# Self-attention on one core: the order of ScalarE's last copies in a unit

## The reference, cut to what matters

```
q, k, v = xn @ Wq1, xn @ Wk1, xn @ Wv1      # 16 heads of 64
attn    = softmax(q k^T * 64**-0.5)         # 512 x 512 for each head
x       = concat_heads(attn @ v) @ Wo1 + bo1 + x
```

## Time and profile before

| | |
|---|---|
| time of 3 runs | 2262.8, 2264.51, 2266.3 us; median 2264.51 |
| profiled execution | 2263.67 us, of which its span (first to last instruction) is 2261.8 us |
| busy share of the span | PE 94%, DVE 71%, ACT 66%, POOL 47% |
| self-attention | about 543 to 1718 us of the span |

### The profile page before, as it was taken

One profiled execution on the slowest core, in us unless ns is written; L12 is line 12 of the kernel. 1 busy time (PEld: TensorE's weight loads), 2 busy tenths in 40 slices (PEclk: granted clock), 3 DMA queues, 4 the chain that ended last, 5 costly groups with the idle time before them and its releaser, 6 DMA issues. The chain is left out here.

```text
span 2261.8 us, 31322 instructions
## 1 busy us (share of the span) xinstructions
PE 2117.4 (94%) x11628; PEld 1768.1 (78%) x11628; DVE 1602.4 (71%) x2349; ACT 1487.3 (66%) x2157; POOL 1066.5 (47%) x830
## 2 busy tenths in 40 slices
PE   6868999998999999999999999999997799999998
PEld 4657888887777777777777777777776788998887
DVE  5576777755787777877877778777785866666553
ACT  5546888766777777777777777777774354555431
POOL 3155444431454454554544545445454666565432
PEclk9979999999999999999999999999999899999999
DMA  6810000021000100001000010010004411111000
GB/s 209 304 44 5 22 22 22 17 76 38 25 15 16 38 15 25 25 15 34 15 25 24 15 34 15 16 34 15 26 29 168 137 58 44 50 57 47 10 10 20
DMA packets 84280, 102.67 MB, mean 45 GB/s; under 512 B 29664, under 2 KB 61152, under 8 KB 83616
## 3 DMA queue, kind: packets, MB, share of 16 engines
q1 hardware_dynamic: 84128, 100.66, 13.5%
HBM read 65.50 MB, written 33.82 MB: 44 GB/s over the span
## 5 line engine op out<-in xcount | busy, mean ns | idle before, releaser
L146 PE MATMUL PS<-R 128*128 128x512 f32 (+1 forms) x2944 | 1021.6, 347 | 60.0 <-DVE R L162 25.1
L147 PE MATMUL PS<-R 128*128 128x512 f32 (+1 forms) x2944 | 994.1, 338 | 0.0
L148 PE MATMUL PS<-R 128*128 128x512 f32 (+1 forms) x2944 | 994.0, 338 | 0.0
L146 PEld LDWEIGHTS PS<-R 128*128 128x128 f32 x2944 | 561.7, 191 | 171.2 <-issue 37.4
L156 ACT ACTIVATE R<-PS 64x512 fp32r<-64x512 f32 (+4 forms) x860 | 460.4, 548 | 230.6 <-PE PS L1840 127.7
L148 PEld LDWEIGHTS PS<-R 128*128 128x128 f32 x2944 | 560.9, 191 | 60.6
L147 PEld LDWEIGHTS PS<-R 128*128 128x128 f32 x2944 | 562.0, 191 | 56.1
L162 DVE TENSOR_TENSOR R<-F,R 128x1024 fp32r<-128x1024 f32 (+2 forms) x418 | 462.9, 1112 | 38.0 <-POOL R L159 22.6
L159 POOL TENSOR_SCALAR R<-F 128x512 fp32r<-128x512 f32 (+1 forms) x293 | 264.0, 903 | 259.5 <-DVE F L1997 147.3
L1535 ACT ACTIVATE F<-PS 128x1024 f32<-128x1024 f32 x256 | 263.0, 1028 | 170.6 <-DVE R L162 112.3
L159 POOL TENSOR_SCALAR R<-R 64x512 fp32r<-64x512 f32 x128 | 142.6, 1129 | 391.3 <-ACT R L156 391.3
(11 more groups left out here) (92 smaller groups left out, 1992.4 us busy)
## 6 DMA issues: line engine op xcount, KB each, us to landing
F<-sd SPq DMA_DIRECT2D x128, 128.0 KB, 2.9
xs<-F SPq DMA_DIRECT2D x16, 512.0 KB, 2.6
F<-xs SPq DMA_DIRECT2D x16, 512.0 KB, 3.5
gd<-F SPq DMA_DIRECT2D x8, 768.0 KB, 3.9
vd<-F SPq DMA_DIRECT2D x8, 768.0 KB, 6.4
R<-gd SPq DMA_DIRECT2D x6, 1024.0 KB, 5.6
R<-vd SPq DMA_DIRECT2D x6, 1024.0 KB, 5.9
F<-in_x SPq DMA_DIRECT2D x8, 512.0 KB, 5.0
```

The lines of the kernel that those rows point to most:

```text
L146: nc.tensor.matmul(o, L[0], Rr[0], start=start, stop=False, skip_group_check=share)
L147: nc.tensor.matmul(o, L[0], Rr[1], start=False, stop=False, skip_group_check=share)
L148: return nc.tensor.matmul(o, L[1], Rr[0], start=False, stop=stop, skip_group_check=share)
```

## The change

ScalarE's two copies of the values' accumulators, with their wait for `o3_lo` of the unit before, move behind the two negating copies of the maxima with theirs. Nothing is added or removed, and no other engine's stream changes.

```diff
                         act_copy(OB[64:65, :], bank(4)[64:65, :])
                         act_copy(OB[0:1, :], bank(5)[0:1, :]).then_inc(d3_sum.sem, 1)
-                        act.wait_ge(o3_lo, d - 1)
-                        act_copy(OA[0:64, :], bank(4)[0:64, :])
-                        act_copy(OA[64:128, :], bank(5)[64:128, :]).then_inc(d3_out.sem, 1)
                     if ok(u, N3) and j == 3:
                         act.wait_ge(nm3_mm, u)
                         act.wait_ge(c3_mm, 4 * (u - 2) + 3)
                         act.wait_ge(k3_clear, u % 2)
                         for h in range(2):
                             m = act_copy(qb[u % 2][h][64:65, :], bank(odd_bank(u))[64 * h:64 * h + 1, :], scale=-1.0)
                         m.then_inc(nm3_neg.sem, 1)
+                    if ok(d, N3) and j == 3:
+                        act.wait_ge(o3_lo, d - 1)
+                        act_copy(OA[0:64, :], bank(4)[0:64, :])
+                        act_copy(OA[64:128, :], bank(5)[64:128, :]).then_inc(d3_out.sem, 1)
```

## The result

| | before | after |
|---|---|---|
| median of the runs | 2264.95 us (4 runs, 2262.8 to 2266.3) | 2291.88 us (4 runs, 2290.51 to 2294.24) |
| ratio | | 1.0115, 95% interval 1.0103 to 1.0127 |
| span of the profiled execution | 2261.8 us | 2288.8 us |

The change costs 27 us, 1.2%. Forecast were 20.5 us, 0.9%. All of it arises in the self-attention: from the second end of a step to the 62nd (60 steps) the timelines take 1108.3 us before and 1135.7 us after.

What follows compares the result with a forecast made beforehand. TensorE was taken to bound the self-attention, VectorE's chain behind E0 being a hidden second bound. Output ends 10.5, late plain ends 9.2 and the rest 0.75 made +20.5 us: 2284.8 us, forecast 2278 to 2292, 8-in-10 range 2268 to 2294.

Steps and rivals of the forecast that it cites:

- What bounds the kernel: Self-attention: TensorE is busy 1099 of 1140 us; VectorE, almost without a pause behind ScalarE's copies, is the hidden second bound.
- The gain at L1385: TensorE's weight load at plain ends waits for ScalarE's maxima; the change can win 0.35 us there.
- Plain ends with late transposes: 20 ends, transposes ending 1.57 to 1.84 us behind the row sums' start: E0 +0.50, TensorE +0.37; 0.46 us taken each.
- margin of L1419: Late plain ends: 0.1 to 0.3 us read between the rests of k and the TensorE matmul that needs them.
- Output ends: 30 ends: `values` +0.24 to +0.37 us on TensorE, E0 +0.36 meeting slack on VectorE's chain; 0.35 us taken each.
- Plain ends with early transposes: 10 ends where ScalarE never idles: TensorE wins 0.4 us and gives it back; 0 to +0.1, 0.05 us taken each.
- The sum: All ends of the self-attention together: 10.5 + 9.2 + 0.75 = 20.5 us slower.
- A: Faster: ScalarE's slack swallows E0's delay; plain ends win 0.35 us each, output ends lose nothing: -11 us, 2254; chance 0.06.
- B: Near nothing: only TensorE's direct wait counts, VectorE's delay of L1419 perhaps meeting a wider margin; +4.4 us, 2269; chance 0.17.
- high end of the sum: E0's shift counts in full at every end: 30 x 0.49 + 20 x 0.62 + 10 x 0.1 = 28.1 us.
- C: Lags add up: `values` and VectorE's chain both cost in each unit, or GpSimd's part moves; +28 to +34 us; chance 0.15.
- The price from the Trainium skill: ScalarE's copies priced by rule at 613 ns, step 520: the two pairs end 0.2 us sooner, estimate about +12 us.

Runs made afterwards that it cites:

- E0: Not a run: ScalarE's work that starts behind the q copies; at late plain ends 4.73 us after the row sums' copies start before, 5.37 in the changed kernel.
- e3_chain: Before, with one more 512-element ScalarE copy (0.6 us) ahead of the q copies behind 58 of the 62 ends; 2299.38 against 2264.39 us.
- e4_direct: Before, with the accumulators' semaphore d3_out raised by the next step's first q copy and no copy moved; 2272.13 against 2264.39 us.
- e5_dve: Before, with the accumulators copied by VectorE in its idle time instead of ScalarE, TensorE also waiting for d3_sum; 2266.99 against 2265.74 us.
- e1_plain: Before, with the change made at the 31 plain ends alone, output ends keeping ScalarE's old order; 2278.54 against 2264.39 us.

## Why the prediction was right, point by point

- **What bounds the kernel.** VectorE's run as the hidden second bound, fed by ScalarE's E0, is what the runs showed; it was underrated. It bounds the steps behind both kinds of ends. The run is not quite unbroken: VectorE waits 0.26 us in each step for ScalarE's copies of v, which move with E0.
- **The gain at L1385.** Came as said (18.8 us of waits to 0.2), and was gone at the next instruction but one.
- **Plain ends with late transposes.** E0 +0.50 foreseen, +0.64 measured; the step +0.46 foreseen, +0.60 measured. Half of E0's missing 0.14 is the accumulators' pair behind the maxima, which takes 1.22 us with its gap and not 1.15 (1014.30 to 1015.52); the other half is the gap ahead of that pair and the lag of the transposes (S+1.68 instead of 1.62), for which the prediction allowed up to 0.12. The step kept 0.60 of 0.64, where the prediction let 0.37 of 0.50 pass. The margin of L1419 that it took off, read from the start of the matmul (1011.79), did not exist: the load had started 0.12 us behind the rests of k in before as well.
- **Output ends.** The step that failed is "+0.36 on VectorE's chain, which here meets slack until the next transposes". There was none, as e3_chain shows. The cost (0.35 foreseen for each, 0.47 measured as the mean) was put on the direct wait of `values`; e4_direct shows that this wait alone is worth 0.13. The size came near by luck: E0's delay here, 0.44, happens to be near that of `values` (0.30 in the stream of matmuls, 0.50 at the load). It was the right size with the wrong carrier.
- **Plain ends with early transposes.** 0.05 foreseen, 0.19 in the mean. TensorE's won time was given back, as said.
- **The sum.** For the 60 steps, 30 x 0.47 + 21 x 0.55 + 9 x 0.19 = 14.1 + 11.6 + 1.7 = 27.4 us (means of the steps after less before), against the foreseen 20.5. The measured 2291.9 lies at the upper edge of the forecast and inside the range up to 2294. All terms were too low, so nothing cancelled in the sum.
- **The rivals.** A is out by e3_chain, in which E0's delay is swallowed at neither kind of end, and e5_dve shows that its gain at L1385 is worth nothing at late plain ends. B is out by e1_plain and e3_chain; its argument, that the waits of before name no L1419 that waited for L1608, rested on a listing that leaves such waits out or calls them "issue". The high end of the sum (28.1, "E0's shift counts in full everywhere") had the mechanism and nearly the time. C added to it that both `values` and the chain cost, which is not so: they overlap.
- **The price from the Trainium skill** (ScalarE: Activation LUTs, What ACT_TABLE_LOAD costs; the two pairs closer packed, about +12 us) would have led away from the result. The rows of this case, 1.19 to 1.22 us for a pair, stand.

## What to carry to other kernels

When a copy is moved behind another on the same engine, ask what it was filling: here it filled the wait for the transposes, and once moved it left that wait idle and came on top of it: E0 came 0.64 us later at late plain ends, and 0.44 at output ends, where other idle time behind it took up a part. Follow the delay along each engine that runs almost without a pause from it, not only to the first one that waits. A wait by several semaphores may be listed as "issue" in the table of waits, and a wait under 0.15 us not at all; compare the start of the instruction with the ends of the work on the other engines before calling it an overhead or slack.

## What the hardware showed that was not expected

A matmul's weight load that waited for one semaphore started 0.05 us behind the end of the work it waited for, whichever engine did that work: L1385 behind ScalarE's maxima in before (1004.65 to 1004.70, and so in all 31 listed waits), L152 behind VectorE's last maximum (31 of 31). One that waited for two or more started 0.11 to 0.12 us behind it: L146 behind the accumulators after the change (1015.50 to 1015.61, and so in all 60 listed waits), L1419 behind the rests of k (1022.35 to 1022.47) and behind L1671 in before (1032.07 to 1032.18, and so in all 30 steps). Since the accumulators' wait is of the second kind and that of the maxima of the first, the change also traded one for the other.
